# A new table of steps for a software-pipelined two-layer transformer kernel

## The reference

```
x = x + ga * attention(layernorm(x) * (1 + ca) + sa)     # 16 heads of 8, 4 key/value groups, relative position term
x = x + gb * experts(layernorm(x) * (1 + cb) + sb)       # 16 experts, 4 chosen per token out of 2 of 4 groups
x = x + ga' * state_space(layernorm(x) * (1 + ca') + sa')  # short convolution, 16-state scan over 256 channels
x = x + gb' * tanh(layernorm(..) @ weight @ aux_weight1 @ aux_weight2 + bias)

attention: softmax(q k' + q E[dist]) v, then Wo
experts:   sum over e of  w_e * (silu(x W1[e] + b1) * (x W3[e] + b3)) W2[e] + b2
state_space: dt = softplus(..);  h_t = exp(dt * A) * h_(t-1) + dt * B_t * x_t;  y = C_t . h_t, times silu(z)
```

## Time and profile before

| | |
|---|---|
| median of 3 runs | 2847.01 us |
| the profiled execution | 2847.01 us, span 2845.2 us |
| TensorE matmul | 2369.1 us busy, 83% of the span |
| TensorE weight load | 1198.3 us, 42% (beside matmuls) |
| VectorE | 1961.8 us, 69% |
| GpSimd | 1821.1 us, 64% |
| ScalarE | 1623.6 us, 57% |
| chain that ended last | PE 45%, DVE 24%, issue 13%, ACT 10%, POOL 6% |
| mean granted TensorE clock | 0.941 |

### The profile page before, as it was taken

One profiled execution on the slowest core, in us unless ns is written; L12 is line 12 of the kernel. 1 busy time (PEld: TensorE's weight loads), 2 busy tenths in 40 slices (PEclk: granted clock), 3 DMA queues, 4 the chain that ended last, 5 costly groups with the idle time before them and its releaser, 6 DMA issues.

```text
span 2845.2 us, 37056 instructions
## 1 busy us (share of the span) xinstructions
PE 2369.1 (83%) x9792; PEld 1198.3 (42%) x9792; DVE 1961.8 (69%) x3116; ACT 1623.6 (57%) x4152; POOL 1821.1 (64%) x2311
## 2 busy tenths in 40 slices
...
GB/s 135 43 58 67 65 138 108 136 105 112 118 125 114 103 125 107 133 109 108 117 125 116 103 126 107 132 114 104 119 121 117 101 121 106 120 87 105 83 123 33
DMA packets 497979, 304.95 MB, mean 107 GB/s; under 512 B 349817, under 2 KB 416297, under 8 KB 497321
## 3 DMA queue, kind: packets, MB, share of 16 engines
...
## 4 chain that ended last, share of the span: by engine, by line
PE 45%; DVE 24%; issue 13%; ACT 10%; POOL 6%; DMA 0%; SPq 0%; ACTq 0%; DVEq 0%; POOLq 0%
PE bank L511 9%; PE bank L820 7%; PE bank L802 5%; DVE work L1066 4%; PE bank L538 3%; DVE zh L816 3%; DVE nmax L518 3%; PE bank L938 2%; PE bank L838 2%; POOL work L1073 2%; PE bank L1085 2%; DVE step L912 2%; PE bank L613 2%; ACT th L809 2%; ACT probs L528 2%
## 5 line engine op out<-in xcount | busy, mean ns | idle before, releaser
L1073 POOL TENSOR_TENSOR work<-work,bc 128x512 f32<-128x512 f32 x512 | 664.0, 1303 | 159.0 <-DVE work L1066 158.6
L1066 DVE TENSOR_TENSOR_SCAN work<-bank,work 128x512 f32<-128x512 f32 x512 | 622.0, 1215 | 173.9 <-POOL work L1060 135.0
L1060 POOL TENSOR_TENSOR work<-work,bc 128x512 f32<-128x512 f32 x512 | 654.5, 1282 | 47.2 <-PE bank L1085 30.4
L833 POOL TENSOR_TENSOR zh<-zh,w_bc 128x512 f32<-128x512 f32 x256 | 325.3, 1271 | 554.7 <-DVE zh L826 554.6
L528 ACT ACTIVATE probs<-bank,nmax 128x256 f32<-128x256 f32 x1024 | 474.2, 471 | 222.8 <-DVE nmax L518 221.9
L1049 ACT ACTIVATE bank<-work,neg_a 128x510 f32<-128x510 f32 x512 | 352.9, 689 | 422.6 <-DVE work L1066 414.7
L511 PE MATMUL bank<-ke,q_all 96*128 96x256 f32 x2048 | 550.7, 392 | 12.0 <-DMA q_all<-q_rows 12.0
L511 PEld LDWEIGHTS bank<-ke,q_all 96*128 96x128 f32 x2048 | 378.8, 195 | 215.1 <-issue 159.1
L518 DVE TENSOR_REDUCE nmax<-bank 128x2 f32<-128x512 f32 x512 | 348.5, 681 | 166.1 <-PE bank L511 153.2
L820 PE MATMUL bank<-h_b,w_t 128*128 128x512 f32 x512 | 288.5, 646 | 117.7 <-DVE zh L816 113.6
L538 PE MATMUL bank<-ident,probs 128*128 128x128 f32 x2048 | 323.7, 282 | 60.6 <-ACT probs_t L546 60.1
...
## 6 DMA issues: line engine op xcount, KB each, us to landing
work<-dt_rows SPq DMA_DIRECT2D x256, 512.0 KB, 5.5
w_bc<-w_rows_d SPq DMA_DIRECT2D x256, 256.0 KB, 4.7
ke<-ke SPq DMA_DIRECT2D x128, 256.0 KB, 4.1
...
q_all<-q_rows SPq DMA_DIRECT2D x512, 8.0 KB
...
```

The costliest lines, as they stand in the source:

```text
L833: nc.gpsimd.tensor_tensor(zh[:, n % 3, :], zh[:, n % 3, :], w_bc[:, n % WB, :], ALU.mult).then_inc(m_p, 1)
L1060: nc.gpsimd.tensor_tensor(hb[at % HB], ring[n % RING][:, 1, :], bc[:, s, :], ALU.mult).then_inc(s_dbx, 1)
L1066: nc.vector.tensor_tensor_scan(hb[at % HB], bank[6][:, :], hb[at % HB], 0.0, ALU.mult, ALU.add).then_inc(s_h, 1)
L1073: nc.gpsimd.tensor_tensor(hb[at % HB], hb[at % HB], bc[:, SG + batch(m)[2], :], ALU.mult).then_inc(s_hc, 1)
```

## The change

Only numbers in the table change: 44 of them move by one to eleven steps, and `FIRST` becomes -102. No instruction is added, removed or altered; many of them move without passing another instruction of their engine. The core of the diff, with all entries that the prediction speaks of:

```diff
-        FIRST, LAST = -112, STEPS * (PAIRS - 1) + 538
+        FIRST, LAST = -102, STEPS * (PAIRS - 1) + 538
...
-            ... x_a_sync=-110, x_res_sync=93, a_store_sync=-29, m_store_sync=182, m_fetch_sync=-9,
+            ... x_a_sync=-100, x_res_sync=104, a_store_sync=-35, m_store_sync=178, m_fetch_sync=-11,
-            m_down_tensor=10,   a_inverse_tensor=41,  a_turned_tensor=-47,  a_query_tensor=-32,
+            m_down_tensor=9,    a_inverse_tensor=42,  a_turned_tensor=-48,  a_query_tensor=-33,
-            f_end_tensor=530,   b_turned_tensor=160,  s_step_tensor=[363, 364],
+            f_end_tensor=531,   b_turned_tensor=159,  s_step_tensor=[364, 365],
-            a_values_scalar=40, a_norm_scalar=-50,    b_turned_scalar=160,
+            a_values_scalar=42, a_norm_scalar=-51,    b_turned_scalar=159,
-            m_up_vector=4,      a_stats_vector=-95,   s_stats_vector=327,   a_root_gpsimd=-86,
+            m_up_vector=3,      a_stats_vector=-88,   s_stats_vector=329,   a_root_gpsimd=-83,
-            m_route_vector=[166, 166, 167, 167, 168, 168, 169, 169, 169, 170, 171, ...],
+            m_route_vector=[166, 166, 167, 167, 168, 168, 169, 169, 170, 170, 171, ...],
```

More of the change, by code:

```diff
@@ new lines, in build @@
+            a_spread_sync=[[-28, -28, -12, 4], [20, 36, 52, 68]], a_scatter_sync=[[-22, 4], [37, 69]], x_a_sync=-100,
+            x_res_sync=104, a_store_sync=-35, m_store_sync=178, m_fetch_sync=-11, s_rows_sync=377,
+            s_rows_in_sync=[378, 380, 384, 386], s_store_sync=[372, 374], s_fetch_sync=-14, f_store_sync=534,
+            a_scores_tensor=0, m_gate_tensor=1, m_up_tensor=3, m_down_tensor=9, a_turn_tensor=5, a_values_tensor=40,
+            a_inverse_tensor=42, s_sum_tensor=6, a_turned_tensor=-48, a_keys_tensor=-42, a_values_in_tensor=-37,
@@ new lines, in build @@
+            a_query_tensor=-33, f_end_tensor=531, a_back_tensor=150, b_turned_tensor=159, m_logits_tensor=164,
+            m_weights_tensor=178, m_back_tensor=326, s_turned_tensor=340, s_in_x_tensor=[348, 356], s_step_tensor=[364, 365],
+            s_rows_tensor=374, s_in_z_tensor=[390, 397], f_out_tensor=508, f_back_tensor=513, f_turned_tensor=524,
+            f_mix_tensor=527, s_decay_scalar=0, m_tanh_scalar=2, a_turn_scalar=8, a_exp_scalar=3, a_values_scalar=42,
+            a_norm_scalar=-51, a_turned_scalar=-42, a_keys_scalar=-40, a_values_in_scalar=-35, a_query_scalar=-33,
@@ L284, in build @@
+            b_norm_scalar=156, b_turned_scalar=159, m_logits_scalar=166, m_weights_scalar=180, m_end_scalar=324,
+            s_norm_scalar=340, s_turned_scalar=342, s_conv_scalar=[351, 359], s_step_scalar=[366, 366], s_rows_scalar=373,
+            s_z_scalar=[391, 399], f_out_scalar=511, f_turned_scalar=526, f_norm_scalar=523, f_mix_scalar=527, s_scan_vector=1,
+            a_max_vector=1, m_up_vector=3, m_silu_vector=2, a_inverse_vector=34, a_scale_vector=42, a_stats_vector=-88,
             a_end_vector=152, b_stats_vector=152,
-            m_route_vector=[166, 166, 167, 167, 168, 168, 169, 169, 169, 170, 171, 171, 172, 172, 173, 173, 174, 174, 175, 175, 176],
@@ L286, in build @@
-            m_end_vector=325, s_stats_vector=327, s_conv_vector=[[349, 349, 350, 350], [357, 357, 358, 358]],
-            s_silu_vector=[352, 360], s_zgate_vector=[392, 401], f_res_vector=515, f_stats_vector=517, f_end_vector=534,
-            s_read_gpsimd=4, m_weigh_gpsimd=5, s_input_gpsimd=-3, a_root_gpsimd=-86, b_root_gpsimd=155, s_root_gpsimd=330,
+            m_route_vector=[166, 166, 167, 167, 168, 168, 169, 169, 170, 170, 171, 171, 172, 172, 173, 173, 174, 174, 175, 175, 176],
+            m_end_vector=327, s_stats_vector=329, s_conv_vector=[[349, 349, 350, 350], [357, 357, 358, 358]],
```

16 lines of the change are left out of this document (2 added, 14 removed).

## The result

The changed kernel takes 2867.22 us (median of 4 runs, 2865.19 to 2869.21) against 2847.19 us of the kernel before beside it (2846.35 to 2848.43): ratio 1.0069, 95% interval 1.0052 to 1.0088. It is 20 us slower; the forecast was 2832. The profiled execution took 2863.71 us with a span of 2861.9; VectorE is busy 1900.0 us instead of 1961.8, TensorE's matmuls 2397.9 instead of 2369.1, and the mean granted clock is 0.938 instead of 0.941. So VectorE did get less to do. The time went elsewhere.

A forecast was written before the change was run, and what follows sets the result against it. VectorE was taken to bound the router stretch from expert 12's m_silu to 14's, TensorE the rest of a pair; the terms summed to -1.26 us per pair, 12 pairs, -15 us: 2847 to 2832, range 2812 to 2866.

The forecast's parts named there:

- at nothing: `b_turned` ahead of the scores: Ahead of expert 12: gate 12 comes later but ScalarE's row hides it, cost nothing; up to 0.86 us without that cover.
- Term 3: At f_mix: m_down ahead of a_inverse lengthens the chain f_mix waits for, +0.5 us a pair, bounds 0 and +0.86.
- Term 4: f_end's transposes go behind expert 10's m_up, so the chain to expert 12 starts earlier: -0.45 us a pair.
- Term 1: VectorE from expert 12's m_silu to 14's: statistics move in, a_root covers four router lines; -2.1, weighted for clock -1.75 us.
- Term 2: Behind expert 14's m_silu: the scan now follows m_up, delaying a_max and expert 15's tanh, +0.94 us a pair.
- Term 5: s_stats behind a scan and a_max, and a_turned's transposes, delay expert 2's scans and gate: +0.45 us a pair.
- term 6: At expert 6: m_down goes ahead of a_turn and fills TensorE's 1.01 us wait for ScalarE, -0.95 us a pair.
- `m_down` ahead of `a_turn` away from expert 6: Priced at nothing: ScalarE takes up a_turn's transposes only behind a tanh and two exponentials, later than 0.86 us.
- The cover misses: Rival: a_root lies beside router steps that gain nothing, VectorE's stretch only takes in the statistics; 2868 us, chance 0.22.
- TensorE becomes the bound: Rival: longer wait for expert 13, then low clock in most pairs, only 0.5 us gained there; 2847 us, chance 0.20.
- Its sign, a low clock in the stretch in most pairs: Sign given for the second rival: a half clock in the stretch from expert 13's m_up to 14's in most pairs.
- an `a_root` held up by short router steps: Possible delay of a_root on GpSimd, some 1 us in all, making -1.1 instead of -2.1; the prediction kept -2.1.

The follow-up runs named there:

- e9: Kernel before with only b_turned moved ahead of the scores, plus two extra TensorE matmuls in the wait ahead of it: 2853.63 us, ratio 1.0016.
- e3: Kernel before with only b_turned moved ahead of the scores (TensorE and ScalarE at 159): 2875.34 us, ratio 1.0089.
- e1: Changed kernel with two extra TensorE matmuls, results overwritten, in the wait ahead of b_turned: 2829.89 us, ratio 0.9931.
- e2: Changed kernel with b_turned alone put back behind the scores (TensorE and ScalarE at 160): 2858.21 us, ratio 1.0033.
- e13: Kernel before with only the moves of Term 1 and Term 2, f_res kept ahead of m_up (514): 2845.90 us, ratio 0.9997.
- e14: e13 with four extra zero-weight matmuls in TensorE's wait ahead of expert 13's m_up: 2844.49 us, ratio 0.9991.
- e7: e1 with Term 5 undone (s_stats_vector 327, a_turned_tensor -47): its prompt for a later run gives 2824 us.
- e8: e1 with m_down_tensor back at 10 and a_inverse_tensor at 41, so m_down behind a_turn again: 70 us off its expectation by the ratios.
- e10: Kernel before with two extra zero-weight matmuls in the wait ahead of expert 13's m_up: 2852.05 us, ratio 1.0009.
- e12: Changed kernel with two extra matmuls ahead of b_turned, and Term 2, Term 4 and Term 5 undone: 2823.19 us, ratio 0.9902.

## Why the prediction was wrong

- **The step that failed** is "at nothing: `b_turned` ahead of the scores makes gate 12 later, hidden by ScalarE's row ahead of tanh 12; without that cover it would cost up to 0.86". In the order of work it was nearly right: in `e9`, where the clock stays up at expert 12, gate 12 starts 38.37 instead of 37.56 us behind gate 8, and `m_silu` 12 at 40.89 instead of 40.88; only `m_silu` 13 follows 0.3 us later. What was left out is the low clock that follows the wait of 1.7 to 1.9 us. The step costs the kernel before 26 us (`e3`), and filling the wait gives the changed one 37 us back (`e1`). The prediction asked after the clock at one place only, behind expert 13.
- That step is not the whole miss. Without it and without filling (`e2`) the sum is still the forecast's 2832, and the time is 2858: terms 3 and 4 cost 0.88 instead of 0.05 us a pair, term 1 gives only -1.15 (L586 takes 1.64 instead of about 1.4 us, and the clock is low behind the wait of 4.15 us), and the end takes 7.7 us more. And that `e1`, at 2830, lies near the forecast is partly luck: L682 and L586 have their short times there, which the prediction did not reckon with, and this pays for terms 3 and 4.
- **Term 1** (-1.75): the four lines took their short times in most pairs; -1.65 in the changed kernel, -1.56 alone (`e13`), -2.25 alone with the clock behind expert 13 filled up (`e14`), where the working had -2.1. So the mechanism is right. That the changed kernel agrees so well is luck: with the filling of `e1` the stretch from `m_silu` 12 to 14 shrinks by 3.23, as L682 and L586 take their short times too (0.21 for 0.98, 0.69 for 1.38), and the low clock takes 1.6 of that away again.
- **Term 2** (+0.94): +0.81 on average, 7.22 instead of 6.12 in a pair whose clock is full there. `m_up` goes first and the scan and `a_max` follow, as the earlier trace rows had to turn out:

```profile
1401.13 0.75 DVE L826 SCALAR_TENSOR_TENSOR zh<-bank,b_c,zh 128x512 f32<-128x512 f32 x1 [1.22 <-PE bank L820]
1401.80 1.21 DVE L1066 TENSOR_TENSOR_SCAN work<-bank,work 128x512 f32<-128x512 f32 x1
```

- **Term 3** (+0.5): `f_mix` comes 0.66 us later within the pair. The delay is there, a little larger than priced.
- **Term 4** (-0.45): wrong sign. The wait ahead of `m_up` 10 was not the chain's last one; it starts where `m_silu` lets it, and 0.4 us of scores and `s_sum` behind `f_end` come later. GpSimd feels it, which had not waited there before:

```profile
1356.45 1.12 PE L820 MATMUL bank<-h_b,w_t 128*128 128x512 f32 x2
1357.41 0.60 PE L405 MATMUL bank<-ident,y_x 128*128 128x128 f32 x4
...
1358.81 1.07 PE L1085 MATMUL bank<-work,sel_d 128*32 128x512 f32 x8
```

```profile
1360.05 1.27 POOL L1060 TENSOR_TENSOR work<-work,bc 128x512 f32<-128x512 f32 x1 [0.33 <-PE bank L1085]
```

  From there `b_root` and `b_norm` come 0.88 us later than before instead of earlier. Terms 3 and 4 together are +0.88 (`e2`) instead of +0.05.
- **Term 5** (+0.45) and **term 6** (-0.95): +0.44 and -0.95. Undoing term 5 gives 0.43 back (`e7`), so it is shown; term 6 was not undone alone, and undone with term 3 (`e8`) its segment grows by 2.08, so its -0.95 agrees but is not isolated. The wait ahead of `a_turn` at expert 6 did not go altogether, 0.60 of 1.01 us are left, but `m_down` lies ahead of it:

```profile
1476.27 1.02 PE L838 MATMUL bank<-zh,w_t 128*128 128x512 f32 x2
1477.88 0.63 PE L538 MATMUL bank<-ident,probs 128*128 128x128 f32 x4 [0.60 <-ACT probs_t L546]
```

- **The sum** took 12 equal pairs and nothing for the start and the end. These read 2.3 and 9.7 us more. The 2.3 are not shown to be a cost, as the start of `e10`, filled only at expert 13, differs from the kernel before by as much (446.3 against 444.2). The end is: a gain that needs the work of four pairs beside each other is not there when the pairs run out, while its price is (6.0 us in `e13`).
- **At nothing** also stood `m_down` ahead of `a_turn` away from expert 6. In the changed kernel it is far from nothing: undone with `a_inverse` (`e8`), the pair is 5.2 us longer, 3.1 of them outside the segment of expert 6, which is more than term 3 gives back. So the move was to the good in this order; why is not shown.
- **The rivals.** "The cover misses" named 2868, and the time came out at 2867; its mechanism is false, the cover hit. "TensorE becomes the bound" had the right cause at the wrong place: the low clock came behind the wait at expert 12, which the prediction took for free. Its sign, a low clock in the stretch in most pairs, came as well: behind expert 13 the clock is low in 10 of 11 pairs of the changed kernel and in 11 of 11 of `e13`, at up to 0.95 us (11.3 against 10.36).
- The Trainium skill (SBUF — State Buffer, Who interferes with whom) was cited for an `a_root` held up by short router steps. In the traces `a_root` takes 4.45 us before and 4.45 us after in nearly all pairs: it was not held up, and -2.1 rather than -1.1 was the better value. The rule's other half, that whichever starts first keeps the other out for the whole instruction, is borne out by the rows of `e12`, but there the one that waits did not always come next: twice GpSimd ran three more operations ahead of it.
